# Half units spread between the full ones, and two output buffers instead of four, in the last expert stage of a decoder kernel

## The reference

```python
scores = sigmoid(layernorm(x) @ gate_w.T)                    # 4096 tokens, 8 experts
choice = two best of (scores + balance_bias)                 # top 2
weight = scores[choice] / (sum(scores[choice]) + 1e-6)
y[token] = sum over its two experts e of
           weight * (silu(row @ w1[e].T) @ w2[e].T)          # 256 -> 512 -> 256
out = x + y
```

## Time and profile before

| | |
|---|---|
| median of three runs | 3260.22 us |
| the profiled execution, its own time | 3260.22 us |
| its span (first to last instruction recorded) | 3258.1 us |
| stage `f` within it | 2963.2 to 3258.1 us |
| mean granted TensorE clock | 0.937 of full |
| weight loads `f_w` | 40 of 1024 KB |
| scatters `out<-f_y,f_token` | 71 |

### The profile page before, as it was taken

The page is one execution under the profiler, slowest core; times in us unless marked ns, Lnnn a source line. Parts: engine busy times, 40 slices in busy tenths (PEclk is TensorE's granted clock), DMA queues, the critical chain, the costliest instruction groups (busy, mean ns, idle before and its releaser), DMA issues.

```text
span 3258.1 us, 49090 instructions
## 1 busy us (share of the span) xinstructions
PE 2730.3 (84%) x16588; PEld 1854.2 (57%) x16588; DVE 1905.0 (58%) x3444; ACT 1522.8 (47%) x2639; POOL 1455.4 (45%) x1633
## 2 busy tenths in 40 slices
PE   6888888876887788868899998699788888866997
PEld 2333333334555466634788885498455555545886
DVE  3878888875887588862122223601689888872111
ACT  4556666634776466520122221344566666642222
POOL 3667767653444577626000005500345555542443
PEclk8999999998999899989899999799899999977998
DMA  9600000000003000012566662200000100005785
GB/s 328 220 1 1 0 1 0 1 0 30 14 13 124 14 1 1 1 38 95 165 212 212 212 205 81 72 1 1 1 14 31 38 31 31 22 27 159 218 217 163
DMA packets 131955, 243.96 MB, mean 75 GB/s; under 512 B 15184, under 2 KB 103376, under 8 KB 121040
## 3 DMA queue, kind: packets, MB, share of 16 engines
q1 hardware_dynamic: 112320, 207.36, 19.6%
q0 software_dynamic: 19440, 34.10, 4.3%
HBM read 154.90 MB, written 87.43 MB: 74 GB/s over the span
## 4 chain that ended last, share of the span: by engine, by line
PE 32%; POOL 6%; issue 6%; DVE 6%; ACT 3%; DMA 2%; another core or an unknown queue 2%; POOLq 1%; SPq 0%; DVEq 0%; ACTq 0%
PE PS L2299 9%; PE PS L2255 4%; PE PS L1886 4%; PE PS L2565 3%; PE PS L2552 3%; POOL e_hs L1445 2%; DMA out<-f_y,f_token 2%; PE PS L1300 1%; POOL rows_in_place L866 1%; POOL e_qs L1448 1%; DVE e_mx L1348 1%; PE PS L1243 1%; PE PS L1877 1%; POOL rows_by_expert L2186 1%
## 5 line engine op out<-in xcount | busy, mean ns | idle before, releaser
L566 POOL TENSOR_TENSOR u_in<-dtx,b_rep 128x512 f32<-128x512 f32 x256 | 325.3, 1294 | 205.9 <-ACT b_rep L547 204.7
L582 DVE TENSOR_TENSOR_SCAN state<-PS,u_in 128x512 f32<-128x512 f32 x256 | 312.4, 1220 | 59.3 <-POOL u_in L566 35.0
L539 PE MATMUL PS<-scaled,ident 128*128 128x512 f32 x512 | 294.8, 660 | 27.4 <-DVE scaled L576 27.3
L2320 ACT ACTIVATE d_act_b<-PS 128x256 f32<-128x256 f32 (+2 forms) x192 | 76.7, 400 | 484.7 <-PE PS L2299 394.3
L1445 POOL TENSOR_TENSOR e_hs<-e_pr 128x512 f32<-128x512 f32 x128 | 162.9, 1273 | 229.5 <-ACT e_pr L1412 227.5
L2332 DVE TENSOR_TENSOR d_hid<-d_act_b,PS 128x256 f32<-128x256 f32 (+2 forms) x192 | 84.4, 441 | 306.6 <-ACT d_act_b L2320 288.6
L2299 PE MATMUL PS<-d_unit_T,d_w 128*128 128x256 f32 (+1 forms) x1280 | 261.8, 358 | 1.0 <-ACT d_unit_T L2309 1.0
L2299 PEld LDWEIGHTS PS<-d_unit_T,d_w 128*128 128x128 f32 x1280 | 222.0, 191 | 26.3 <-issue 1.4
L555 ACT ACTIVATE PS<-dt,decay_rate 128x508 f32<-128x508 f32 x256 | 173.4, 686 | 132.9 <-DVE state L582 131.1
L576 DVE TENSOR_TENSOR scaled<-state,PS 128x512 f32<-128x512 f32 x256 | 169.5, 665 | 60.8 <-PE PS L520 49.1
L2615 POOL DMA_INDIRECT out<-f_y,f_token x71 | 110.3, 1553 | 186.5 <-DVE f_token L2599 125.3
(11 more groups left out here) (451 smaller groups left out, 6385.1 us busy)
## 6 DMA issues: line engine op xcount, KB each, us to landing
d_w<-in_d_w SPq DMA_DIRECT2D x42, 1024.0 KB, 5.0
f_w<-in_f_w SPq DMA_DIRECT2D x40, 1024.0 KB
rows_in_place<-blank SPq DMA_DIRECT2D x136, 272.0 KB, 5.2
d_w<-in_d_w SPq DMA_DIRECT2D x42, 512.0 KB, 3.9
rows_by_expert<-zeros SPq DMA_DIRECT2D x36, 256.0 KB, 2.8
f_unit_rows<-rows_in_place SPq DMA_DIRECT2D x31, 272.0 KB, 5.3
d_unit_rows<-rows_by_expert SPq DMA_DIRECT2D x31, 256.0 KB, 4.1
out_by_expert<-d_y_rows SPq DMA_DIRECT2D x31, 256.0 KB, 4.1
```

Of the source, the lines that this page charges most:

```text
L539: nc.tensor.matmul(YB[:, c], ident[:], scaled[:, (KD * n + c) % RC], start=False, stop=n == NS - 1).then_inc(m_y, 1)
L566: nc.gpsimd.tensor_tensor(u_in[:, k % RU], dtx[:, p, c], b_rep[:, n % RB], ALU.mult).then_inc(m_u, 1)
L582: nc.vector.tensor_tensor_scan(state[:, k % 2], DECAY[:, k % RD], u_in[:, k % RU], 0.0, ALU.mult, ALU.add).then_inc(m_h, 1)
```

## The change

1. `unit_plan` no longer puts the half units last. After every third or fourth full unit it puts one half unit: behind full units 3, 6, 10, 13, 17, 20, 24, 27 and 30 (numbered from 0). The numbers of the units' places, from which the table is computed, go with them. Counts stay: 31 full, 9 half.
2. `y` has 2 buffers instead of 4, and `token` 3. The waits on `added` follow: before DVE writes `y` of unit u, unit u-2 must have been added (before: unit u-4); before it writes `token`, unit u-3 (before: unit u-4).

```diff
 def unit_plan(groups):
     full, single = split_units(groups)
-    return [(2, 2 * n) for n in range(full)] + [(1, 2 * full + n) for n in range(single)]
+    kinds, done = [], 0
+    for n in range(full):
+        kinds.append((2, 2 * n))
+        if (n + 1) * single // full > done:
+            kinds.append((1, 2 * full + done))
+            done += 1
+    return kinds
...
-        RING, OUT = 3, 4
+        RING = 3
...
-        y = t("y", [128, OUT, UT, D])
-        mine, share, token = t("mine_rows", [128, UT, E]), t("share_rows", [128, UT]), t("token", [128, OUT, UT], I32)
+        y = t("y", [128, 2, UT, D])
+        mine, share, token = t("mine_rows", [128, UT, E]), t("share_rows", [128, UT]), t("token", [128, RING, UT], I32)
...
-                after(dve, added, 16 * late(u - OUT + 1))
-                nc.vector.tensor_copy(token[:, u % OUT, 0:n], rows[:, r, 0:n, D + E]).then_inc(sent_to, 1)
+                after(dve, added, 16 * late(u - RING + 1))
+                nc.vector.tensor_copy(token[:, r, 0:n], rows[:, r, 0:n, D + E]).then_inc(sent_to, 1)
...
-                after(dve, added, 16 * late(u - OUT + 1))
+                after(dve, added, 16 * late(u - 1))
                 for k in range(n):
                     dve.wait_ge(down, upto[u] + k + 1)
-                    nc.vector.tensor_scalar(y[:, u % OUT, k], DB(k), share[:, k:k + 1], None, ALU.mult).then_inc(mixed, 1)
+                    nc.vector.tensor_scalar(y[:, u % 2, k], DB(k), share[:, k:k + 1], None, ALU.mult).then_inc(mixed, 1)
...
-                    nc.gpsimd.indirect_dma_start(tokens_of, bass.IndirectOffsetOnAxis(token[:, u % OUT, k:k + 1], 0), y[:, u % OUT, k], None,
+                    nc.gpsimd.indirect_dma_start(tokens_of, bass.IndirectOffsetOnAxis(token[:, u % RING, k:k + 1], 0), y[:, u % 2, k], None,
```

## The result

| | before | changed |
|---|---|---|
| median on one chip, four runs each | 3260.51 us (3260.15 to 3263.35) | 3289.53 us (3280.98 to 3295.37) |
| profiled execution, its own time | 3260.22 us | 3287.47 us |
| its span | 3258.1 us | 3285.3 us |
| from the first scatter of stage `f` to the end of the span | 277.2 us | 309.2 us |

The changed kernel takes 1.0085 times as long as the one before (95% interval 1.0068 to 1.0101): 29 us more. The forecast was 3281, with a range of 3245 to 3297.

The account below looks back on a forecast made before the run. PE paces the full units and the chain of scatters ends the span; 3244.1 us at PE's pace plus 35 of collisions gives a span of 3279, plus 2.1 a time of 3281 us, range 3245 to 3297.

Parts of the forecast that it names:

- The sign and the mechanism: Last stage: slower, as loads just behind scatters lengthen them, DVE waits for landings and PE for DVE; 3281 us.
- The price of a group: 3.44 full units and one half unit take 33.8 us instead of 29.1: 4.7 more, 7.5 times, 35 us.
- Two of 3.44 long pairs in a group: Per half unit, two full units' scatter pairs meet a load at 9.5 us each; the other 1.44 take 6.9.
- the pair behind each half unit is free: Half unit's short second product brings its load 1.7 us sooner, so the next pair of scatters meets no load.
- The half unit's own scatter: First half unit: next load 0.7 us behind its scatter, a second collision, next issue at 3019.8; in the sum 4.9.
- The state keeps itself up: Scatters set the pace; while a full unit takes over 7.33 us, PE waits and its load stays behind the pair.
- The waits of DVE: DVE's `f_y` waits for the landing of `out` some 10 to 20 times, over 20 us in sum.
- The term at PE's pace: Stage end if PE never waits: span 3244.1 against 3258.1, a gain of 14.0 us.
- A: Last stage: PE keeps the pace and the gain is whole, 3246 us; chance 0.23.
- B: Last stage: one collision of load and scatters in a group, 3262 us, no change that can be told; chance 0.12.
- C: Last stage: nearly all full units collide, the two buffers throttle it throughout, 3310 us; chance 0.05.
- The load at 3020.2: Weight load running over unit 5's pair, to about 3024.5; with 2.7 us for the pair, its landing is 3027.2.

Follow-up runs that it names:

- one half unit spread: Changed kernel's two buffers for `y`, but one half unit behind full unit 3 and the other eight at the end; 1.0002 to before.
- the gate: Changed kernel, SP's weight load of unit u waiting for the first tile's landing of u-4, two semaphores: 0.9978 to before; the same in the old order: 1.0002.
- small loads: Weight loads from the fourth unit on bring 128 KB instead of 1024: changed kernel so altered 0.9958 to before, kernel before so altered 0.9970.
- half units first: Changed kernel's two buffers for `y`, but all nine half units ahead of the 31 full ones; 1.0014 to before.

## Why the prediction was right, and where it was off

- **The sign and the mechanism held.** A load behind a pair makes the pair long (8.53 us from the second scatter at the first half unit, forecast 7.6), DVE waits for the landing, and PE waits for DVE (25.2 us). Without the loads' bytes, or with the loads put elsewhere, the loss is gone (0.9958, 0.9978). The last scatter was at 3278.8, forecast 3272.
- **The price of a group was too low.** Forecast 4.7 us over PE's pace, 7.5 times, 35 in all. Measured 309.2 - 263.2 = 46, 5.8 for each of 8, or 5.3 without the 3.5 us of unit 33, which nothing in the forecast stood for. The span was off by less (3285.3 against 3279), because the stage happened to begin 4.8 us sooner; that is luck. The median time was off by 8.5 us.
- **Which units pay was partly wrong.** Two of 3.44 long pairs in a group was the right count, but they are the one two ahead of the half unit (10.5, taken as 9.5) and the one right behind it (8.8), which I had called free. The free one is right ahead of it (6.7). The step that failed is "the pair behind each half unit is free": I followed the load relative to a PE that is one unit ahead, and in the steady state PE is two ahead. That the count came out at two is luck, since its reason was wrong. The half unit's own scatter was said to collide at the first half unit and took 5.93; in the sum it stood at 4.9 and measured 5.8.
- **"The state keeps itself up" is wrong** with two buffers. One half unit's disturbance fades within two or three units, though DVE goes on waiting. In the changed kernel the next half unit comes before or as it has faded. With four buffers the load does stay at one place from unit 12 to unit 32, and full units take 8.6 to 10.6 us; whether one half unit alone would bring that about was not run. The sum happened to need only what two bad pairs in a group cost, so the error did not show in it.
- **The waits of DVE**: 33 times and 210.8 us, against 10 to 20 times. The forecast treated them as the loss; they carry the lag and cost nothing by themselves (one half unit spread: 198.7 us, a ratio of 1.0002).
- **The buffers.** I took the two buffers as part of the harm, since they let PE be throttled. They halve it: the same order with four is at 1.0188. Why four are worse was seen (load and scatters in step) but not tested.
- **The term at PE's pace**, 14 us of gain, is real only when loads and scatters are kept apart (266.5 against 279.3 with the gate). With small loads the old order has it as well.
- **Rivals.** A (PE keeps the pace, 14 us of gain) is near what the gated version does (266.5 against 263.2 of stage), not the changed one. B and C are out by time and by the pairs: 3262 and 3310, with two long pairs in a group.
- **Slips in the working.** The load at 3020.2 would run to 3024.7 and the pair to 3027.4, not 3024.5 and 3027.2. POOL waited last for DVE in 30 of its waits, not 27 (3 more behind `f_y`). The 0.65 for "slower" leaves out the tenth of the forecast that was said to fall below 3266. None of these changes the sum. The earlier trace rows was read too strongly: its window begins with the scatter's own issue, and with small loads the scatter issued at 3111.12 moved no packet before 3113.1 either, yet 142 by 3114.54. So about 2 of the 3.4 us are the scatter's own start, and only the rest is the load in its way.

## What to carry to other kernels

When two chains share the transfer engines, look not at their shares but at which transfer is issued behind which: here a load of 1024 KB just behind a pair of small scatters made it 10.5 us long, one well ahead of it 7.2, none nearby 6.5. A reordering that evens out one engine's work moves the other engines' transfers too; follow each transfer one group further than the first, in the state that the waits have brought about. A large sum of waits is a symptom: take it as a cost only when the pace has changed beside it.

## What the runs showed that I had not expected

- Loads with packets a quarter as long leave the loss as it is (1.0107), though the scatter then gets twice as many packets through beside the load. In the changed kernel a scatter and a load moved 89 and 129 packets in the same 3 us, so it is slowed and not shut out.
- Unit 33 takes 11.7 us in the changed kernel, and 10 to 13 in the versions with the spread order, except the one gated at the first tile (7.6). Its second scatter is issued late at POOL itself:

```profile
3242.71 1.55 POOL L2621 DMA_INDIRECT out<-f_y,f_token  x1 [3.76 <-issue]
```

That is 5.3 us behind the first instead of 1.86. It is the issue behind the 60th scatter of the stage, in the kernels with one half unit spread (unit 30) and half units first (unit 34) too. Instruction fetches stand in the traces near this moment, but in the changed kernel none lies between the two scatters. The cause stays open.
